# A two-layer attention and mixture-of-experts kernel: order of steps made by a greedy planner, and layer-1 scores and maxima in 64-row halves of the array

## The reference

```python
# layer 0
x = layernorm(x + attention0(x))          # 8 heads of 16, causal, w_qkv, w_out; a rank-1 term is added to the scores
# layer 1
h = x + mla_attention(rmsnorm(x))         # 16 heads of 8, causal, k and v from a normed latent of 64, rotary q and k
y = h + moe(rmsnorm(h))                   # 4 experts 128 -> 512 -> 128, all computed, the one with the largest gate kept
x = layernorm(x + y)
```

## Time and profile before

| | us |
|---|---|
| three runs: median (lowest, highest) | 675.29 (673.31, 678.19) |
| the profiled execution: its device time | 673.76 |
| its span, first to last instruction | 671.9 |
| outside the span (673.76 - 671.9) | 1.9 |
| PE, DVE, ACT, POOL busy in the span | 582.0, 413.1, 337.8, 145.5 |
| mean granted clock of TensorE | 0.954 of 2.4 GHz |

### The profile page before, as it was taken

One profiled execution on the slowest core, in us unless ns is written; L12 is line 12 of the kernel. 1 busy time (PEld: TensorE's weight loads), 2 busy tenths in 40 slices (PEclk: granted clock), 3 DMA queues, 4 the chain that ended last, 5 costly groups with the idle time before them and its releaser, 6 DMA issues.

```text
span 671.9 us, 10096 instructions
## 1 busy us (share of the span) xinstructions
PE 582.0 (87%) x3668; PEld 279.0 (42%) x3717; DVE 413.1 (61%) x1031; ACT 337.8 (50%) x621; POOL 145.5 (22%) x186
## 2 busy tenths in 40 slices
PE   5578899958777877879999999999989999799994
PEld 3224233424223233424433344455544545357663
DVE  3496987796615968897778878754566402422313
ACT  4234457544463454557766667545546555633330
POOL 7612112313371031135321214011012011101000
PEclk9798899978787998999999999999999999989997
DMA  4856020000044020031313030220000000000000
GB/s 141 210 159 219 26 73 25 2 1 0 32 116 75 1 65 0 3 64 48 85 28 60 6 65 0 31 35 1 2 0 18 2 0 1 17 0 1 17 1 16
DMA packets 27394, 27.69 MB, mean 41 GB/s; under 512 B 6289, under 2 KB 22545, under 8 KB 27090
## 3 DMA queue, kind: packets, MB, share of 16 engines
q1 hardware_dynamic: 26962, 26.26, 16.2%
q0 software_dynamic: 384, 0.79, 0.5%
HBM read 19.40 MB, written 7.34 MB: 40 GB/s over the span
## 4 chain that ended last, share of the span: by engine, by line
PE 64%; DVE 20%; DMA 4%; issue 4%; ACT 4%; POOL 2%; SPq 1%; DVEq 0%; ACTq 0%; POOLq 0%
PE ps L875 13%; PE ps L948 10%; PE ps L858 10%; DVE mparts L1238 10%; PE ps L837 9%; PE ps L1004 8%; PE ps L834 3%; PE ps L937 3%; PE ps L931 2%; ACT pr L1024 2%; DMA qs<-nparts 2%; PE ps L912 2%; PE ps L946 2%; PE ps L886 1%; DVE stats L1147 1%
## 5 line engine op out<-in xcount | busy, mean ns | idle before, releaser
L1024 ACT ACTIVATE pr<-ps 128x512 f32<-128x512 f32 (+1 forms) x456 | 250.3, 576 | 227.9 <-PE ps L858 192.1
L1238 DVE TENSOR_REDUCE mparts<-ps 128x1 f32<-128x512 f32 (+3 forms) x456 | 279.9, 655 | 112.4 <-PE ps L837 111.2
L837 PE MATMUL ps<-ks,qs 125*128 125x512 bf16 (+3 forms) x576 | 170.0, 337 | 12.6 <-DVE mparts L1238 11.1
L858 PE MATMUL ps<-qs,ks 128*128 128x512 bf16 (+3 forms) x532 | 154.6, 332 | 15.7 <-ACT pr L1024 9.2
L752 POOL TENSOR_SCALAR_AFFINE_SELECT pr<-pr 128x512 f32<-128x512 f32 x96 | 61.0, 636 | 369.1 <-ACT pr L1024 368.9
L875 PE MATMUL ps<-pr,vs 128*32 128x512 f32 (+3 forms) x1152 | 126.4, 512 | 0.4 <-POOL pr L752 0.4
L858 PEld LDWEIGHTS ps<-qs,ks 128*128 128x128 bf16 x576 | 50.8, 99 | 143.2 <-ACT pr L1024 92.5
L834 PE MATMUL ps<-cmask,identb 128*128 128x128 bf16 (+2 forms) x259 | 64.9, 251 | 26.9 <-DVE mparts L1238 12.5
L837 PEld LDWEIGHTS ps<-ks,qs 125*128 125x128 bf16 x576 | 55.4, 100 | 53.1 <-DVE mparts L1238 21.2
L948 PE MATMUL ps<-w,work 128*128 128x128 f32 x512 | 74.1, 288 | 0.0
L1089 ACT ACTIVATE work<-ps,b 128x512 f32<-128x512 f32 x64 | 43.8, 686 | 49.1 <-PE ps L1004 48.5
(11 more groups left out here) (119 smaller groups left out, 391.5 us busy)
## 6 DMA issues: line engine op xcount, KB each, us to landing
qs<-scr1q SPq DMA_DIRECT2D x64, 64.0 KB
ks<-scr1k SPq DMA_DIRECT2D x64, 64.0 KB
qs<-scr0q SPq DMA_DIRECT2D x48, 64.0 KB, 2.3
ks<-scr0k SPq DMA_DIRECT2D x36, 64.0 KB, 2.2
scr0q<-parts SPq DMA_DIRECT2D x4, 384.0 KB, 2.8
scr0k<-parts SPq DMA_DIRECT2D x4, 384.0 KB, 3.2
scr1q<-parts SPq DMA_DIRECT2D x4, 384.0 KB, 2.5
scr1k<-parts SPq DMA_DIRECT2D x4, 384.0 KB, 2.6
```

The costliest lines, as they stand in the source:

```text
L837: last = pe.matmul(bank[:, h, :], queries(F, KMAX, h0 + h, i * P, P), ks[0:KMAX, F % SLOTS, h0 + h, 512 * c:512 * c + w], start=not diagon ...
L858: last = pe.matmul(to[:, h, :], ks[0:KEXP, F % SLOTS, h0 + h, j * P:(j + 1) * P], queries(F, KEXP, h0 + h, qb * 512 + lo, n), start=True, ...
L1024: act.activation(pr[:, st % PSLOTS, h0:h0 + nh, 0:STEPS[st][3]], scores_at(F, v), ACT.Exp, scale=GROUPS[F][0].scale).then_inc(exped, 1)
L1238: dve.tensor_reduce(mparts[:, F % SLOTS, h0:h0 + nh, i, c], maxes_at(F, u), AX_X, ALU.max).then_inc(taken, 1)
```

## The change

**Halves.** In layer 1 the products go from 8 to 6, which makes 48 rows a head, and with the maximum's three rows they fit in 64. Heads 0 and 1 of a group go to rows 0 to 63 and heads 2 and 3 to rows 64 to 127, so each layer-1 `max` or `scores` matmul uses one half of the array's rows. Loads take two DMAs of 32 KB per product instead of one of 64 KB, and the maxima's rows take six DMAs instead of three. The mask of a diagonal block takes two matmuls (128 and 64 columns a head) instead of one (128). A unit holds at most 2 heads (before: 4), so a group has 40 units of each kind instead of 38. Heads are listed 0, 2, 1, 3 for the scores and 2, 0, 3, 1 for the maxima.

**Order.** `backbone`, the hand-written positions of chains and `spread`'s weights go. In their place, `wanted()` gives each step a rough position in one of many lanes, and `order()` takes, one at a time, the lane head with the smallest (expected wait of its engine in us + position), by a table of durations. It knows PSUM banks, semaphores and free engines, and when both halves of the array are busy. For `max` steps it looks up to six ahead for one in the half not used last.

**Chains.** `between` goes by 512-row block, not by sequence. The first RMS norm needs no square and sum any more: its root is computed from the layer norm's variance (`hat0` on DVE), beside the layer norm's own root in the same instructions. Layer norm's own result `x1` moves to POOL (four instructions a block).

```diff
-ATT = [..., Attention(1, 8, [(0, 0), (0, 1), (1, 0), (1, 1), (0, 2), (2, 0), (1, 2), (2, 1)], 8 ** -0.5)]
+PRODUCTS = [(0, 0), (0, 1), (1, 0), (1, 1), (0, 2), (2, 0)]
+ATT = [Attention(0, 16, PRODUCTS, 16 ** -0.5), Attention(1, 8, PRODUCTS, 8 ** -0.5)]
+HALF = P // 2
+HEADS = [0, 2, 1, 3]
...
-        nh = min(HG, 512 // n)
-        out += [(s, h, nh) for h in range(0, HG, nh)]
+        nh = min(2, 512 // n)
+        out += [(s, h, nh) for h in HEADS if h % nh == 0]
...
+        base, first = HALF * (h // 2), h % 2 * T + lo
+        return qs[base:base + HALF - MAXIMA + more, F % SLOTS, first:first + n]
...
-    out += spread(between(0), *BETWEEN[0]) + loads(BETWEEN[0][1], 4)[1:] + loads(BETWEEN[0][1], 5)
-    out += spread(between(1), *BETWEEN[1])
-BETWEEN = [(2.21, 3.12), (4.21, 5.95)]
-AFTER = (8.21, 11.7)
-LAST = (11.71, 12.4)
+FIRST = [[(-2.0, -1.5), (-1.6, -1.1)], [(-0.5, 0.0), (-0.1, 0.4)]]
+BETWEEN = [[(1.2, 1.21), (2.0, 2.01)], [(3.4, 4.9), (4.1, 5.6)]]
+READY = [[(7.4, 7.9), (8.1, 8.4)], [(11.4, 11.6), (12.1, 12.2)]]
+EXPERTS = [[(7.9, 9.7), (9.7, 11.4)], [(11.6, 13.0), (13.0, 14.0)]]
+HOP = 0.07
+AFTER_ISSUE = {PE: 0.17, DVE: 0.0, ACTE: 0.0, POOL: 0.0, SP: 2.2}
+URGENT = 1.0
...
+    if kind == "scores":
+        st, _, nh = UNITS[step[2]]
+        cols = nh * STEPS[st][3]
+        return [(PE, cols / 2400 + 0.01 * nh), (ACTE, 0.17 + cols / 1180)]
+    if kind == "max":
+        i, c, _, nh, w = MAXES[step[2]]
+        masked = (512 * c + w == (i + 1) * P) * nh * (128 if GROUPS[step[1]][0].n == 0 else 192)
+        return [(PE, (masked + nh * w) / 2400 + 0.01 * nh), (DVE, 0.1 + nh * w / 880)]
+    if kind == "pv":
+        return [(PE, 0.16 + 0.00165 * STEPS[step[2]][3])]
...
+                same_half = [k for k in range(left) if (waiting[k][1][2] < NX0) == (waiting[0][1][2] < NX0)]
+                picks = [k for k in same_half if last_tile not in halves_of_array(waiting[k][1])][:1] or [0]
+            for k in picks:
+                at = ready(waiting[k][1], shared)
+                if at is not None:
+                    best.append((at[0], waiting[k][0], name, k, at[1]))
+        _, pos, name, k, at = min(best, key=lambda x: max(x[0], 0.0) + URGENT * x[1])
...
+            if engine == PE:
+                own = halves_of_array(step) if kind in ("scores", "max") else (0, 1)
+                issued = time + cost if len(own) == 2 else time
+                for t in own:
+                    tile_free[t] = time + cost
...
+                if at.n == 1:
+                    for pair_of in range(2):
+                        first = HALF * pair_of + j * at.hd
...
+                    low, high = ((identb, cmask), (identx, cmaskx))[::-1 if h0 // 2 else 1]
+                    pe.matmul(bank[:, :, w - P:w], low[0][own, :], low[1][own, 0:nh, :], start=True, stop=False,
+                              skip_group_check=True)
+                    pe.matmul(bank[:, :, w - HALF:w], high[0][own, :], high[1][own, 0:nh, HALF:P], start=False, stop=False,
+                              skip_group_check=True)
...
+                elif kind == "hat0":
+                    b, i = args
+                    dve.wait_ge(done["root"], nth("root", "x1", b, (i,), 3))
```

More of the change, by code:

```diff
@@ L324, in experts, with ready @@
+def ready(b, i):
+    return [("feed", "att1", b, i), ("feat", "att1", b, i), ("y", 1, b, i), ("residual", 1, b, i),
+            ("square", b, i), ("square_sum", b, i), *root("rms1", b, (i,)), ("hat", b, i), ("x12", b, i),
+            ("feed", "hat1", b, i), ("feat", "hat1", b, i), ("gate", b, i), ("pick", b, i)]
 def experts(b, i):
@@ L338 @@
           "gate": "pick", "hidden": "relu", "expert": "pick_up"}
-LONG = {"layer_norm": 1.5, "hat": 2.0, "lat_norm": 2.0, "moments": 1.5, "pick": 1.5}
 def spread(steps, first, last):
-    total, passed, out = sum(LONG.get(s[0], 1.0) for s in steps), 0, []
-    for s in steps:
-        out.append((first + (last - first) * passed / total, s))
-        passed += LONG.get(s[0], 1.0)
-    return out
-def loads(position, F):
-    if F >= ATT[0].groups:
-        return [(position, ("load", F, k, 2)) for k in range(2)]
-    return [(position, ("load", F, k, i)) for i in range(2) for k in range(2)]
@@ L383, with halves_of_load, wanted, add @@
-SECOND = (-0.5, 0.4)
-BETWEEN = [(2.21, 3.12), (4.21, 5.95)]
-AFTER = (8.21, 11.7)
-LAST = (11.71, 12.4)
-SCHEDULE = schedule()
+    return [(first + (last - first) * k / len(steps), s) for k, s in enumerate(steps)]
+def halves_of_load(F):
+    return (0, 1) if F in HALVED else (2,)
+def wanted():
+    out = [(pos, "attention", s) for pos, s in attention() + maxima_steps()]
+    def add(stream, steps):
+        out.extend((pos, stream, s) for pos, s in steps)
+    for b in range(B):
+        for i in range(2):
+            add(("first", b, i), spread(before_first(b, i), *FIRST[b][i]))
+            add(("before", b, i), spread(between(b, i), *BETWEEN[b][i]))
+            add(("after", b, i), spread(ready(b, i), *READY[b][i]))
+            add("result", spread(experts(b, i), *EXPERTS[b][i]))
+    for F in range(NF):
+        for half in halves_of_load(F):
+            add("loads", [(max(-1.05, F - 1.9) + 0.01 * half, ("load", F, k, half)) for k in range(2)])
+    add("loads", [(F - 0.5, ("copy_v", F)) for F in range(NF)])
+    add("once", [(0.05, ("weights",)), (0.6, ("b2_parts",)), (0.7, ("partners",)), (1.2, ("halves",)),
+                 (-1.99, ("pads", 0)), (-1.98, ("pads", 1)), (-0.62, ("pads", 2)), (NF + 0.9, ("quiet",))])
+    add("once", [(F - 2, ("ones", F)) for F in range(ATT[0].groups, ATT[0].groups + SLOTS)])
+    return out
@@ new lines, with lane @@
+OWN_LANE |= {kind: kind for kind in ("hidden", "relu", "expert", "pick_up", "x1", "x12", "scores", "pv", "mask", "copy_v", "quiet",
+                                     "pads", "ones", "halves", "weights", "b2_parts", "partners")}
+def lane(stream, step):
+    kind = step[0]
+    if kind in ("max", "load"):
+        return step[:4] if kind == "load" else step[:2]
+    if kind in ("hi", "r1", "mid", "lo", "store"):
+        return "split", step[1]
+    if kind in ("proj", "rotate", "rotated", "v_proj", "v_out"):
+        return OWN_LANE[kind], step[1] >= (8 if OWN_LANE[kind] == "projections" else 1)
+    return OWN_LANE.get(kind, stream)
@@ L390, in plan @@
+SCHEDULE, ENDS = order(wanted())
+MAX_ORDER = [[s[2] for s in SCHEDULE if s[:2] == ("max", F)] for F in range(NF)]
 def plan():
@@ L800, in _ @@
                     continue
-                before[:] = [done[kind], {"pads": 2}.get(kind, 1) * nth(*step)]
+                before[:] = [done[kind], {"ones": 4, "pads": 2}.get(kind, 1) * nth(*step)]
         @block.tensor
```

692 lines of the change are left out of this document (462 added, 230 removed).

## The result

The changed kernel takes 649.85 us (median of 4 runs, 644.48 to 651.31) beside 676.15 us for the kernel before (4 runs, 673.31 to 678.19): ratio 0.9599, 95% interval 0.9532 to 0.9667. It is 4% faster; the prediction said 10% (608 us, range 574 to 655). Executions over 1.5% above the fastest of their kernel are left out of its ratio (one of run 1's four; run 2 has three such of four, and no ratio).

The account below looks back on a forecast made before the run. PE was taken to bound the kernel almost everywhere, with stretches that nothing fills between. Forecasts stretch by stretch summed to 604.5 us of span, plus 1.9 outside, 606.4; predicted 608 us, range 574 to 655.

Parts of the forecast that it names:

- groups 2 and 3 under 100 us: Sign to look for: groups 2 and 3 with layer 1's chain, 117.1 us before, forecast at 95.
- The last two stretches together: Groups 8 to 11 and the experts behind the attention: 172 and 80 us forecast, 188.7 and 86.6 before.
- 21 less 8: Groups 8 to 11: PE's busy 178 us falls to 157 by halved scores and maxima, then 8 of hops make 165.
- 80 new hops: Experts beside attention: changes between layer-1 and full-array tile shapes, 0.1 us each, 8 us in all, bounds 0 and 32.
- The estimate of 5.6 us a group: Layer-1 scores and maxima: side estimate of the halves' gain, 18.4 to 11.9 us, not used in the sum.
- the gain of 6.0 us a group: Layer-1 scores and maxima: halves 75% overlapped cut PE's 18.4 us to 11.5, leaving a need of 22.5 a group.
- A layer-1 group without other work is then DVE's at 24 us: Groups 6 and 7: with PE's need at 22.5 us, DVE's reduces set the pace at 24 us a group.
- 7 us of waits: Groups 6 and 7: added to DVE's 2 x 24 us for a stretch of 55, 62.7 before.
- 3 to 5 us if a group's rows queue behind a load: Layer-1 loads on SP: cost if rows arrive late just before a group's first scores; otherwise hidden.
- The order misfits: Rival, 16%: wrong table prices make early-listed instructions block queues; groups 2 to 5 gain a third, hops cost 16: 639 us.
- Halves don't run together: Rival, 12%: layer-1 matmuls of different halves do not overlap, and groups 4 to 11 lose 45 us: 653 us.
- The clock rival: Rival, 9%: PE pauses in groups 4 to 11 bring half clock for 40% of its work there: 698 us, slower.

Follow-up runs that it names:

- run 1: Changed kernel with the three DMAs of the experts' weights issued behind the second bias's parts: 643.49 us, ratio 0.9512.
- run 2: Changed kernel, same order, but both pairs of heads in rows 0 to 63, so no layer-1 matmuls can run together: 725.58, 746.12, 750.13 and 752.71 us.
- run 5: Changed kernel with layer 1 in full rows (six products, one mask) and the planner told, the order alone: 654.69 us, ratio 0.9685.
- run 7: As run 1, with the planner's price of `rows` set to 3.7 us in layer 1 and 1.85 in layer 0: 636.38 us, ratio 0.9419.
- after: The changed kernel itself, beside the kernel before: 649.85 us, ratio 0.9599.
- run 9: Changed kernel with layer 1 in full rows, the experts' weights issued later and `rows` priced as traced: 648.88 us, ratio 0.9606.
- run 6: Changed kernel with three PSUM banks for scores and two for maxima, instead of two and three: 695.11 us, ratio 1.0255.
- run 11: As run 7, with a hop between PE's tile shapes priced at 0.09 us in the planner's table: 629.97 us, ratio 0.9323.
- 10: As run 7, with four banks for maxima instead of three and one for projections and experts instead of two: 635.69 us, ratio 0.9408.
- 12: As run 11, with four maxima banks and one side bank up to group 8's first maxima, then three and two: 615.25 us, ratio 0.9093.
- run 8: As run 7, with the table's prices for exponentials and maxima reduces set by distances between starts: 638.42 us, ratio 0.9441.
- run 4: Kernel before, with its hand-written order and chains, and only the halves put in: 710.56 us, ratio 1.0523.

## Why the prediction was wrong, point by point

**What held.** The direction; halves run together; a hop costs 0.1 us; groups 2 and 3 under 100 us (89.1); ACT's waits for PE down, 192 to 157. The last two stretches together (255.6 for 252) are in part luck, since some 6 us of their work moved into group 7.

**The halves, from group 8 on: about right.** To see this I summed, over groups 8 to 11, the distance from each matmul's start to the next one's (what exceeds its columns at 2.4 GHz by 0.25 us I counted as waiting), in run 5 and in run 7:

| | run 5, full rows | run 7, halves |
|---|---|---|
| scores, maxima, masks | 40.3 + 24.2 + 4.6 = 69.1 | 27.3 + 17.2 + 5.1 = 49.6 |
| experts | 73.9 | 77.3 |
| `pv` | 36.2 | 36.2 |
| other | 9.8 | 11.3 |
| waits | 6.0 | 9.1 |

The layer-1 steps save 19.5 us. Hops into the experts and other steps and waits give back 8.0, and 11.5 stay (11.2 by the lengths, 194.7 to 183.5). The forecast had 21 less 8. It took 80 new hops here; run 7 changes the tile shape 82 times more than run 5 (253 and 171). The estimate of 5.6 us a group that rested on the Trainium skill (TensorE: Matmul & The Clock Gate, Part 3: Packing small matmuls) is borne out in these groups: 19.5 us over four groups of scores and three of maxima, 3.5 groups, are 5.6 each. The Trainium skill's sentence that changing the tiling mode drains TensorE (TensorEngine Tiling (Array Packing), Key Properties) is borne out at 0.1 us a hop. The stretch as a whole is 13.8 us over its 172 because it holds more: by the same sum the expert steps in it take 82 us in after and 68 before, and the last stretch has them less. The forecast's 165 us of PE at the density it names would also be 175, not 172.

**The halves in groups 4 to 7: the step that failed.** The forecast took the gain of 6.0 us a group there as well, by "A layer-1 group without other work is then DVE's at 24 us", plus 7 us of waits, 55 for two. From run 9 to run 7 the halves changed groups 4 and 5 by 0.3 us and groups 6 and 7 by 3.0. Group 6 is the clean case, with no other work, no half clock and no pause for rows. Run 9, then run 7:

```profile
315.70:346.90 31.20, 30.27 (x224) 12.18 (x225) 25.15 (x50) 21.72 (x44) 5.47 (x9) 1.00 0.17 27
316.94:347.10 30.16, 28.11 (x247) 10.39 (x246) 24.60 (x50) 21.41 (x43) 5.50 (x9) 1.00 0.10 28
```

The halves gave 1.0 us, not 6.0 of PE's need or 3.8 of time (31.3 to 27.5). Summed as in the table above, scores, maxima and masks take 20.0 us there without halves and 18.3 with them, where I had 11.5. Two things keep them up. Their distances fall short of their columns at 2.4 GHz by 5.4 us in all, which is what ran beside a partner; the forecast had 6.9, and from group 8 on it is 6.3 a group. And where the distances exceed the columns, the excess (small waits, and hops among them) grew from 3.6 to 6.2 us. DVE is busy 24.6 us, near the forecast's 24, but the time beside it is 6 us in this one group, where I priced waits of 7 for two: that term is the mis-sized one. That these waits come from handing banks over (three for maxima, two for scores) is what I take from ACT and PE waiting for each other in turn (17.8 and 17.0 us in groups 6 and 7 of after, run 6). Two maxima banks make it worse (run 6), but a fourth hardly helps: group 6 takes 30.2 and 28.7 us with three banks (runs 7 and 11) and 28.7 and 28.4 with four (runs 10 and 12). So the cause of the waits in group 6 is argued, not shown.

**Rows and the clock: not in the sum.** The prediction had "3 to 5 us if a group's rows queue behind a load" and left it out. Rows were late three times: 12.6 us in group 0, behind a load that stood at a store, and 2.7 and 2.4 in groups 4 and 5. Near each of these there are 10 to 14 us at half clock; only the first two began within the pause. Moving three transfers and pricing `rows` took 12 us off (ratios 0.9599 and 0.9419). The clock in groups 4 and 5 was 0.89, under my 0.9. Of their 14.5 us over the forecast these mends took back 4.6 (90.5 to 85.9). The rest stayed: DVE is busy 72.7 us there, as before (72.4), and PE's waits and the half clock of group 5 were no terms of the 76.

**The order: half of what I took.** Of the forecast's 67 us I had given some 27 to the halves and 40 to order and chains. The order alone gave 21 (run 5), with both mends 27 (run 9: 0.0394 of 675.4). Groups 1 to 3 took 137.5 us for 126.5: I counted PE's need and a clock of 0.95, and the ring of maxima held it up there. A fourth bank takes 7.4 us off under 7's table (134.5 to 127.1) and 7.5 under 11's (130.8 to 123.3). The clock goes with it, 0.97 with three and 1.00 with four, but 6.8 us at half clock can cost 3.4 at most. With two banks it is 153.7, at 0.90.

**The rivals.** "The order misfits" (639, 16%) comes nearest by its mechanism: an instruction that the table lists early blocks its queue. Of the two prices it named, the reduce's was harmless (run 8) and the hop's was worth some 6 us (run 11, with intervals that overlap); wrong were also the prices of `rows` and of a store's landing (2.2 us, taking 9.8 and then 4.7). By its number "Halves don't run together" (653) is nearer still, but that is chance: its mechanism did not happen. With the order's table mended and banks moved, the same halves and chains reach 615.25 us, 7 above the forecast. That does not confirm the forecast's terms: the end is 12 us under its 80 and groups 0 to 3 are 4 under, while groups 4 to 11 are 27.5 over.

The clock rival (698 us) did not come: the mean clock is 0.95, as before.

**Parts do not add.** The halves without the new order cost 5.2% (run 4), the order without them gives 3.15% (run 5), both together 4.0%.

**Open.** Run 2's clock, and what brings the clock down in group 5 with the rows in time. What the waits in groups 4 to 7 come from. Run 4's loss was not split between hops, landings and clock.
